# Two attend products to a head, with a value tile that holds both halves, in a gated cross-attention and expert block

## The reference

```python
# cross-attention and its MLP, 16 heads of 16
q = (x @ Wq + bq); k = (y @ Wk + bk); v = (y @ Wv + bv)      # split into heads
scores = jnp.einsum('bnhd,bmhd->bhnm', q, k) * scale
attn = jax.nn.softmax(scores, axis=-1)
out = jnp.einsum('bhnm,bmhd->bnhd', attn, v).reshape(B, N, IMAGE_DIM)
h = jax.nn.relu(out @ W1 + b1)
return h @ W2 + b2
# experts, 8 of them, the two best of each token
scores = jnp.maximum((x @ gate_W + gate_b) / TEMP, EPS)
p = jax.nn.softmax(scores, axis=-1)
...
comb = jnp.where(topk_mask, w, jnp.zeros_like(w))
y = jnp.einsum('bsd,edf->bsef', x, expert_W) + expert_b
out = jnp.einsum('bsef,bse->bsf', y, comb) / K
# the block
x = x + jnp.tanh(g_xattn[0]) * xattn(layernorm(x), ctx_768, ...)
x = x + jnp.tanh(g_ffn[0]) * ffn(layernorm(x), ...)
```

## Time and profile before

| | |
|---|---|
| median of 3 runs | 954.12 us (953.99 to 955.93) |
| profiled execution | 955.33 us, span 953.5 us |
| TensorE busy | 919.9 us, 96% of the span |
| VectorE busy | 809.1 us, 85% |
| ScalarE busy | 719.6 us, 75% |
| GpSimd busy | 633.1 us, 66% |
| chain that ended last | TensorE 91%, issue 3%, VectorE 2%, GpSimd 2%, ScalarE 1% |
| mean granted clock of TensorE | 0.973 |

### The profile page before, as it was taken

One profiled execution on the slowest core, in us unless ns is written; L12 is line 12 of the kernel. 1 busy time (PEld: TensorE's weight loads), 2 busy tenths in 40 slices (PEclk: granted clock), 3 DMA queues, 4 the chain that ended last, 5 costly groups with the idle time before them and its releaser, 6 DMA issues.

```text
span 953.5 us, 26162 instructions
## 1 busy us (share of the span) xinstructions
PE 919.9 (96%) x9410; PEld 669.3 (70%) x9410; DVE 809.1 (85%) x2108; ACT 719.6 (75%) x1517; POOL 633.1 (66%) x793
## 2 busy tenths in 40 slices
PE   4789999999999999999999999999999999999997
PEld 2566777777777777777777777777777777777763
DVE  5776988888988888898888889888888988888876
ACT  4756878877787877778787777778777878877661
POOL 5545776667677666767766767866676776667643
PEclk8578999999999999999999999999999999999999
DMA  6100000000000000000000000000000000000000
GB/s 206 29 15 1 27 27 16 26 26 19 21 26 25 17 27 26 13 27 27 15 26 26 26 13 26 27 15 27 26 26 13 27 26 16 26 13 13 13 13 23
DMA packets 17615, 24.61 MB, mean 26 GB/s; under 512 B 2814, under 2 KB 9168, under 8 KB 17488
## 3 DMA queue, kind: packets, MB, share of 16 engines
q1 hardware_dynamic: 17488, 22.94, 7.7%
HBM read 14.54 MB, written 8.39 MB: 24 GB/s over the span
## 4 chain that ended last, share of the span: by engine, by line
PE 91%; issue 3%; DVE 2%; POOL 2%; ACT 1%; POOLq 0%; DVEq 0%; ACTq 0%
PE e L755 33%; PE g L755 19%; PE t L939 9%; PE t L804 6%; PE s L890 4%; PE g L956 3%; PE s L827 3%; PE s L828 3%; PE s L826 2%; PE g L764 2%; PE g L901 2%; PE g L966 1%; PE t L924 1%; PE g L845 1%; PE g L836 1%
## 5 line engine op out<-in xcount | busy, mean ns | idle before, releaser
L381 POOL TENSOR_TENSOR p_lo<-p_f,p_hi 77x512 f16<-77x512 f32 x161 | 187.8, 1182 | 82.8 <-ACT p_hi L570 82.8
L755 PE MATMUL e<-we_hi,x2T_lo 128*128 128x512 f16 x496 | 189.4, 382 | 0.0
L755 PE MATMUL e<-we_lo,x2T_hi 128*128 128x512 f16 x496 | 189.1, 381 | 0.0
L755 PE MATMUL e<-we_hi,x2T_hi 128*128 128x512 f16 x496 | 188.9, 381 | 0.0
L1233 DVE SCALAR_TENSOR_TENSOR acc<-e,comb,acc 128x256 f32<-128x256 f32 x307 | 146.6, 478 | 27.4 <-PE e L755 24.0
L569 ACT ACTIVATE p_f<-t 77x512 f32<-77x512 f32 x256 | 152.3, 595 | 15.5 <-PE t L804 8.6
L570 ACT ACTIVATE p_hi<-t 77x512 f16<-77x512 f32 x256 | 152.2, 595 | 0.0
L1283 DVE TENSOR_REDUCE row_max<-s 128x6 f32<-128x462 f32 (+1 forms) x192 | 108.0, 577 | 7.6 <-PE s L890 5.2
L365 POOL TENSOR_TENSOR ve<-mv,ln_eps 128x1 f32<-128x1 f32 x64 | 14.6, 227 | 141.8 <-DVE mv L1334 141.8
L826 PE MATMUL s<-v_hi,p_lo 77*128 77x17 f16 x1024 | 98.1, 172 | 5.2 <-POOL p_lo L381 5.1
L826 PEld LDWEIGHTS s<-v_hi,p_lo 77*128 77x128 f16 x1024 | 84.1, 97 | 25.4 <-issue 10.6
(11 more groups left out here) (195 smaller groups left out, 2859.8 us busy)
## 6 DMA issues: line engine op xcount, KB each, us to landing
x_sb<-in_x SPq DMA_DIRECT2D x32, 256.0 KB, 2.7
out<-acc SPq DMA_DIRECT2D x31, 256.0 KB, 2.0
we_f<-in_L_ffn_expert_W SPq DMA_DIRECT2D x2, 1024.0 KB, 9.6
y_sb<-in_ctx SPq DMA_DIRECT2D x32, 57.8 KB
w_f<-in_L_xattn_W SPq DMA_DIRECT2D x2, 512.0 KB, 7.3
wq_f<-in_L_xattn_Wq SPq DMA_DIRECT2D x1, 256.0 KB, 4.1
out<-acc SPq DMA_DIRECT2D x2, 128.0 KB, 1.7
wkv_f<-in_L_xattn_Wk SPq DMA_DIRECT2D x1, 192.0 KB, 2.9
```

The costliest lines, as they stand in the source:

```text
L381: pool.tensor_tensor(p_lo[:, r].rearrange("m h n -> m (h n)"), p_f[:, r, :], p_hi[:, r].rearrange("m h n -> m (h n)"), ALU.subtract).then_ ...
L755: mm = pe.matmul(out_ap, a, c, start=(first and i == 0), stop=(last and i == n - 1))
```

## The change

The two value tiles `v_hi` and `v_lo` become one, `v_both`, of 33 columns a head: 16 of the high part, the column of ones, 16 of the low part. For 15 of the 16 heads and tiles of a half, attend is two matmuls of 33 columns, `p_hi` by `v_both` and `p_lo` by `v_both`; the 16th would pass the bank's end and keeps three, of 17, 16 and 17 columns. The low part's products now stand in 16 columns of their own: ScalarE copies them for each half to a new tile `low_values` (`low_values_copy`), and VectorE adds this to the high columns in the bank (`add_low_values`) ahead of the reciprocals. The product with both low parts is summed as well, which the kernel before leaves out.

On GpSimd both key blocks stand ahead of `stack_comb`, and the first waits for VectorE's `p_low(m, 7)`. On TensorE the transposes of the combination move behind expert 1, and both bias products behind the key stack's transposes. At s = 32 expert 6 of row f moves from ahead of attend 3 to ahead of attend 1, and expert 5 of row e, so far at the start of s = 33, to the end of s = 32.

```diff
+PACK = DV + DH
+PACKED = T * H // 2 - 1
...
-        v_hi, v_lo = sb("v_hi", [M, 2, H, DV], F16), sb("v_lo", [M, 2, H, DV], F16)
+        v_both = sb("v_both", [M, 2, H, PACK], F16)
...
+        low_values = sb("low_values", [P, 2, PACKED, DH])
...
             def key_blocks(b, c):
 
                 pool.wait_ge(khT_done, b + 1)
+                if b > 1 and c == 0:
+                    pool.wait_ge(p_lo_vector, len(VECTOR_LOW) * b - 1)
...
                 if has(s, 0):
                     key_blocks(b, 0)
+                if has(s, 0):
+                    key_blocks(b, 1)
                 if has(s, -2):
                     stack_comb(e, eu)
                 if has(s, 0):
-                    key_blocks(b, 1)
                     k_low(b)
...
+            def low_values_copy(b, half):
+                act.wait_ge(av_done, 8 * b + 4 * half + 4)
+                at_least(act, low_values_added, 2 * (b - 1) + half + 1)
+                parts = S[half][:, 0:PACKED * PACK].rearrange("p (a d) -> p a d", d=PACK)
+                act.activation(low_values[:, half], parts[:, :, DV:PACK], ACT.Copy).then_inc(low_values_copied, 1)
...
                 if front:
                     highT_copies(b)
+                if mid:
+                    low_values_copy(m, 0)
+                if front:
                     q_stack_high(b)
+                if mid:
+                    low_values_copy(m, 1)
+                if front:
                     k_stack_high(b)
...
-                        dst = S[half][:, at:at + DV]
-                        pe.matmul(dst, lo, v_hi[:, u, h, :], start=True, stop=False)
-                        pe.matmul(dst, hi, v_lo[:, u, h, :], start=False, stop=False)
-                        mm = pe.matmul(dst, hi, v_hi[:, u, h, :], start=False, stop=True)
+                        if a < PACKED:
+                            dst = S[half][:, a * PACK:(a + 1) * PACK]
+                            pe.matmul(dst, hi, v_both[:, u, h, :], start=True, stop=False)
+                            mm = pe.matmul(dst, lo, v_both[:, u, h, :], start=False, stop=True)
+                        else:
+                            dst = S[half][:, a * PACK:a * PACK + DV]
+                            pe.matmul(dst, lo, v_both[:, u, h, 0:DV], start=True, stop=False)
+                            pe.matmul(dst[:, 0:DH], hi, v_both[:, u, h, DV:PACK], start=False, stop=False)
+                            mm = pe.matmul(dst, hi, v_both[:, u, h, 0:DV], start=False, stop=True)
...
-                if last and s <= B + 1:
+                if last and s <= B:
                     experts(f, fu, 5, s - 3, (lambda: transposes_y(pair, b, u)) if front else None)
...
+                if s == B:
+                    experts(f, fu, 6, s - 3)
+                if mid:
                     attend(m, mu, 1)
...
-                if last:
+                if last and s != B:
                     experts(f, fu, 6, s - 3)
...
-                if first and s <= B:
-                    combT_transposes(e, eu)
                 if front:
                     scores_for_max(b, 1)
                 if first and s <= B:
                     experts(e, eu, 1, s - 2)
-                    expert_biases(e, 0)
+                    combT_transposes(e, eu)
                 if front:
                     scores_for_max(b, 2)
-                if first and s <= B:
-                    expert_biases(e, 1)
...
                 if front:
                     key_stack_transposes(b)
+                if first and s <= B:
+                    expert_biases(e, 0)
+                    expert_biases(e, 1)
...
+            def add_low_values(b, half):
+
+                dve.wait_ge(low_values_copied, 2 * b + half + 1)
+                parts = S[half][:, 0:PACKED * PACK].rearrange("p (a d) -> p a d", d=PACK)
+                dve.tensor_tensor(parts[:, :, 0:DH], parts[:, :, 0:DH], low_values[:, half], ALU.add).then_inc(low_values_added, 1)
...
                 if mid:
+                    add_low_values(m, 0)
                     reciprocals(m, 0)
                     normalise(m, 0, 0)
                     normalise(m, 0, 1)
                 if mid:
+                    add_low_values(m, 1)
                     reciprocals(m, 1)
```

More of the change, by code:

```diff
@@ L47 @@
 EARLY = 7 + 5
-CONSTS = EARLY + 1 + 8
+CONSTS = EARLY + 1 + 7
 PARTS = 4
@@ L207, in gated_block @@
         av_done = sem("av_done")
+        low_values_copied = sem("low_values_copied")
+        low_values_added = sem("low_values_added")
         rden_done, o_done = sem("rden_done"), sem("o_done")
@@ L448, in _ @@
             pool.memset(kz[:], 0.0).then_inc(consts_ready, 1)
-            pool.memset(v_hi[:, :, :, DH:DV], 1.0).then_inc(consts_ready, 1)
-            pool.memset(v_lo[:, :, :, DH:DV], 0.0).then_inc(consts_ready, 1)
+            pool.memset(v_both[:, :, :, DH:DV], 1.0).then_inc(consts_ready, 1)
             pool.memset(graw[:, :, E:E + 1], EPS).then_inc(consts_ready, 1)
@@ L1099, in step @@
                     experts(e, eu, 4, s - 2)
+                if s == B:
+                    experts(e, eu, 5, s - 2)
                 if mid:
@@ L1258, in q_high @@
                 dve.tensor_copy(q_hi[:], q[:]).then_inc(q_hi_done, 1)
+            def add_low_values(b, half):
+                dve.wait_ge(low_values_copied, 2 * b + half + 1)
+                parts = S[half][:, 0:PACKED * PACK].rearrange("p (a d) -> p a d", d=PACK)
+                dve.tensor_tensor(parts[:, :, 0:DH], parts[:, :, 0:DH], low_values[:, half], ALU.add).then_inc(low_values_added, 1)
             def reciprocals(b, half):
                 dve.wait_ge(av_done, 8 * b + 4 * half + 4)
-                src = S[half][:, 0:T * (H // 2) * DV].rearrange("p (t h d) -> p t h d", t=T, h=H // 2)
-                dve.reciprocal(rden[:, half], src[:, :, :, DH]).then_inc(rden_done, 1)
+                dve.reciprocal(rden[:, half].rearrange("p t h -> p (t h)"), S[half][:, DH:512:PACK]).then_inc(rden_done, 1)
             def normalise(b, half, t):
@@ L1268, in normalise @@
                     dve.wait_ge(rden_done, 2 * b + half + 1)
+                    dve.wait_ge(low_values_added, 2 * b + half + 1)
                     if half == 0:
                         at_least(dve, oT_in_psum, b)
-                src = S[half][:, 0:T * (H // 2) * DV].rearrange("p (t h d) -> p t h d", t=T, h=H // 2)
+                corner = S[half][:, t * (H // 2) * PACK:t * (H // 2) * PACK + DH]
+                src = bass.AP(corner.tensor, corner.offset, [corner.ap[0], [PACK, H // 2], [1, DH]])
                 dve.tensor_tensor(o[:, t, half * P:(half + 1) * P].rearrange("p (h d) -> p h d", h=H // 2),
-                                  src[:, t, :, 0:DH],
+                                  src,
                                   rden[:, half, t, :].unsqueeze(2).to_broadcast([P, H // 2, DH]),
```

6 lines of the change are left out of this document (3 added, 3 removed).

## The result

The changed kernel takes **967.61 us** (median of 4 runs, 967.17 to 968.98), against 954.27 us for the kernel before in the same batch (4 runs): a ratio of 1.0137, 95% interval 1.0124 to 1.0150. It is slower by 1.4%, as forecast (967.3 us, range 946 to 978). The profiled execution took 968.98 us, its span is 967.3 us.

A forecast was written before the change was run, and what follows sets the result against it. TensorE binds the 27.91 us step; -0.76 products, -0.10 key-block wait and +1.35 new waits make +0.49 us. Over 29 steps +14.2, end -1.0: 955.33 becomes 968.5, less 1.2 for the median 967.3 us, range 946 to 978.

The forecast's parts named there:

- The attend products: TensorE's attend: 30 fewer matmuls a step at 25 ns each, 33 columns costing what 17 do, saving 0.76 us.
- Where the saving stops: Expert 7 and attend 7: waits for VectorE's adds and p_low(m, 7) leave 0.39 us of the 0.76 there.
- The copies and adds: ScalarE's new copies take 0.47 us, VectorE's new adds 0.40 us, ahead of the last o.
- The transposes of `o`: TensorE's load for them comes at 529.38 instead of 529.08, 0.30 us later, behind VectorE's second add.
- Expert 1 and the biases: Expert 1 starts at 530.30 after expert 7's adds; bias products wait 0.20 us for combT; mlp_up at 532.70.
- the key block's wait: TensorE's wait for GpSimd's second key block, 0.10 us a step on the matmuls, goes with the reordering.
- The end: Last steps: expert 6 moved ahead of attend 1 gives back 1.9 us, partly lost to a copy and add: -1.0 us.
- The first steps: First two steps, half warm-up: put at nothing, with a share that could be 1 us either way.
- The clock: Rival: TensorE's new pauses bring a half-clock stretch in every step, 1.7 us x 29, 1017 us; chance 0.02.
- The shorter hand-over: Rival: load for o at 528.95, no bias or key-block wait, step 0.23 us shorter, 946 us; chance 0.15.
- the saving lands whole: Rival: 0.86 us saved in every step, 928 us, needing the last o done by 528.3; chance 0.05.
- evens out: Rival: step equal to within 0.1 us, total within 0.2% of before, 954 us; chance 0.10.

The follow-up runs named there:

- the first two runs: Changed kernel without the copies and adds, 960.58 us; kernel before with the changed orders and GpSimd's wait but three products, 963.76 us.
- the last kernel above: Changed kernel with maxima chunk 1 behind expert 1, norm statistics ahead of the second maximum, and the end of the kernel before: 957.88 us.
- half 0 alone: The last kernel above, but with two products, copy and add only in half 0 and three products in half 1: 944.48 us.
- Three runs: Changed kernel with orders of before, without GpSimd's wait, 984.9 us; same with three products in half 1, 977.9 us; changed kernel without that wait only, 1038.12 us.

## Why the prediction was right

**The attend products.** 25 ns for 33 columns, as taken.

**Where the saving stops.** Right in kind. VectorE's stretch from `yT_lo` to `p_low(m, 7)` did not follow TensorE; it is 8.27 us and not 8.37, because VectorE's `gfloor` takes 0.49 us (at 527.73 above) instead of 0.59 (at 522.39 in the kernel before); why it does is not traced. ("Shorter than 8.4 us" was to count against the forecast; by this tenth it is, and it changed no term by more.) This puts `p_low(m, 7)` 0.10 us earlier than assumed. The wait that the prediction split between expert 7 and attend 7 is all but 0.02 us ahead of expert 7 (load idle 0.18 us). Expert 0's load comes 0.46 us earlier than before (11.26 us into the step against 11.72, medians), so that much of the 0.76 was left there, and not 0.39.

**The copies and adds.** The add was taken at 0.40 us and 0.33 to the next start; it is 0.40 to 0.42 and 0.32. The copy was taken at 0.47 and 0.35 from the 128x256 row; it is 0.38 and 0.25, at the `combT` end of the bounds. That copy 1 comes only behind `q_stack` was right, and the run with it ahead priced that at 0.13 us a step.

**The transposes of `o`.** Forecast +0.30 us, measured +0.14. The difference is copy 1, which is what the second add waits for: it starts 0.07 us earlier than walked, behind the shorter copy 0, and takes 0.09 us less.

**Expert 1 and the biases.** The wait at expert 1 was to be 0.08 us and shows as 0.32 in the load's row, because what stood ahead was done sooner; expert 1 starts at 535.47 - 5.34 = 530.13, forecast 530.30. The wait for `combT` is 0.19 us, forecast 0.20. `mlp_up` is at 532.64, forecast 532.70.

**The step.** +0.49 forecast, +0.45 measured, 13.0 us of the 13.8 in 29 steps (forecast 14.2). The runs confirm the parts as causes: without copies and adds 0.25 us comes back, with the orders alone 0.28 is lost, and with one copy earlier 0.13 comes back. One term had only half its reason: the block's new place doesn't remove the key block's wait by itself. With the same order and an earlier `o` (the first two runs) the wait is there; it is gone from the changed kernel because `o` comes later as well.

**The end: the step that failed.** "Moved ahead of attend 1, it lies in a wait. That gives back 1.9 us", with -1.0 us in the sum. Measured is +2.12 us, of which the move itself is +1.15. The other 0.97 us goes with the new orders: the new orders with three products and the old end have 48.39 us (with 6.8 us at half the clock instead of 3.4), and the last kernel above, with every copy and add, the old end and the other order, has 46.59, less than the 46.86 before. So the 0.87 us charged for a copy and an add isn't seen either (46.59 us with them in both halves, 46.61 with half 0 alone). How the orders cost what they do there is not traced. The error is that ScalarE's wait at 916.97 was read as what bound the end. What bound the start of expert 7 was the add of expert 5 on VectorE, at a fixed distance from `scores(m, 0)`: the same argument as in the steady step, not made there. And the half-clock stretch did not vanish with the work in it; here it fell on the next.

**The first steps.** Put at nothing, measured -1.42 us (95.73 against 97.15). This one says little: the changed kernel with the old end has the same program up to there and took 94.07. The errors of the sum are -1.2 us in the steps, -1.4 in the first ones and +3.1 in the end: that the total came out within 0.5 us of the profiled execution is luck, since its parts did not.

**What the prediction didn't see.** It read the 1.70 us of a key block as a cost to GpSimd and costed GpSimd's wait for what it delays. Three runs show that VectorE can be the one held, for 1.2 or 2.4 us ahead of attend 7. Without that wait the change would have cost 70 us more.

**The rivals.** The clock stayed at 1.00 over the 29 steps, with 0.44 us a step in which no matmul ran. The shorter hand-over did not come: it would have needed the load of `o` at 528.95, and that was at 529.22. Its hope that `p_low(m, 7)` gets shorter once no key block runs beside it failed, because what holds it there is GpSimd's `p_lo`, which runs as before: 0.74 us. That the saving lands whole, or evens out, is ruled out by a step 0.45 us longer.

## What to carry to other kernels

When work of the engine that binds is cut, first find the chains on other engines that start at the step's beginning: what waits for them stays where it is, so cut only as much as they let through (here half of the products), keep new copies and adds out of the hand-over, and look again at what is late next. A line that makes one engine wait for another may guard a third, so take it out alone before judging its cost, and read the lengths of the instructions beside it and not only the waits. Work moved at the end of the program has to be judged by the chain that binds there, like any other.

## What the runs showed of the hardware

- A VectorE subtraction of 77x512 with both inputs in SBUF takes 0.68 us alone, 0.74 us when it starts 0.19 us ahead of the end of a GpSimd subtraction, 1.95 us when one GpSimd key block goes ahead of it as well and 3.17 us with two in a row. In each of the held cases it ends 0.55 us behind the last GpSimd instruction that held it: the wait goes into the instruction's length, and the list of waits names only who waits for it. GpSimd's next instruction, back to back with the one that runs, can go ahead of a VectorE instruction that has started 0.155 us earlier; at the same distance the kernel before has the opposite outcome in each step.
- A ScalarE copy of 128x240 from PSUM takes 0.38 us, 0.25 to the next start; a VectorE add with one input and the output in PSUM, 0.40 to 0.42 and 0.32. The groups of the changed kernel, whole span:

```profile
L1292 DVE TENSOR_TENSOR s<-s,low_values 128x240 f32<-128x240 f32 x64 | 26.2, 409 | 4.3 <-ACT low_values L615 3.3
...
L615 ACT ACTIVATE low_values<-s 128x240 f32<-128x240 f32 x64 | 24.4, 381 | 5.7 <-PE s L852 5.7
```

- Steady steps in which the loads wait 0.6 us at one place and 1.3 us in all keep a clock of 1.00; the wait of 1.91 us at the end was followed by 3.4 us at 0.50. A wait of 2.4 us in each of 29 steps was followed by such a stretch in two of them, with TensorE busy for 1.14 and 1.59 us of the 3.4 us ahead of the fall.
